# A two-layer transformer kernel on one core: the first stage's normalised tiles, latents' weights, weight splits and gate buffers are put in another order

## The reference, cut to what matters

```python
xn = _layernorm(x, axis=-1)                       # no weights
# attention latents (192 + 64 + rope columns), then a layernorm of each
q_latent = _layernorm(xn @ q_a_w.T, ...)
kv_mixed = xn @ kv_a_w.T
# feed-forward: rms norm of xn, router (32 experts, top 4), shared part
x2 = w_norm * (xn * rsqrt(mean(xn * xn) + eps))
logits = x2 @ w_router
sh = silu(x2 @ sw_gate) * (x2 @ sw_up) @ sw_down  # 704 hidden columns
```

## Time and profile before

| | |
|---|---|
| Time, median of 3 runs | 721.2 us (719.69 to 723.97) |
| The profiled execution | 723.6 us, its span 721.8 us |
| PE / PEld | 687.2 us (95%) / 583.5 us (81%) |
| DVE / ACT / POOL | 498.0 (69%) / 404.5 (56%) / 284.6 us (39%) |
| PE in 0 to 8.8 us and 8.8 to 11.5 us | 0.00 and 1.92 us busy |
| PE in 67 to 107 us | 39.84 us busy |

### The profile page before, as it was taken

One profiled execution on the slowest core, in us unless ns is written; L12 is line 12 of the kernel. 1 busy time (PEld: TensorE's weight loads), 2 busy tenths in 40 slices (PEclk: granted clock), 3 DMA queues, 4 the chain that ended last, 5 costly groups with the idle time before them and its releaser, 6 DMA issues.

```text
span 721.8 us, 13707 instructions
## 1 busy us (share of the span) xinstructions
PE 687.2 (95%) x4708; PEld 583.5 (81%) x4708; DVE 498.0 (69%) x1440; ACT 404.5 (56%) x1062; POOL 284.6 (39%) x289
## 2 busy tenths in 40 slices
PE   4999999999999999998999979999979999999997
PEld 2677888888888888887876655666779999999997
DVE  5798877877868778777884895777555454644544
ACT  2666158788788878788112565888753322222221
POOL 0473245556465454631004208998233230400000
PEclk9999999999999999999999986999999999999999
DMA  8902034453534444352800000200300000000000
GB/s 319 334 0 82 16 108 133 150 169 113 174 114 164 128 141 136 101 156 93 360 0 1 1 2 1 103 2 2 118 1 1 2 1 15 1 15 1 2 16 15
DMA packets 26724, 59.42 MB, mean 82 GB/s; under 512 B 3146, under 2 KB 12748, under 8 KB 26272
## 3 DMA queue, kind: packets, MB, share of 16 engines
q1 hardware_dynamic: 23584, 50.35, 20.7%
q0 software_dynamic: 3072, 8.20, 3.4%
HBM read 48.24 MB, written 10.49 MB: 81 GB/s over the span
## 4 chain that ended last, share of the span: by engine, by line
PE 75%; DVE 15%; ACT 5%; issue 3%; DMA 1%; POOL 1%; SPq 0%; DVEq 0%; ACTq 0%
PE bank L2155 10%; PE bank L1935 7%; PE bank L1869 6%; PE bank L1926 5%; PE bank L2204 5%; PE bank L2178 5%; PE bank L1955 3%; PE bank L1876 3%; PE bank L1946 3%; PE bank L2066 3%; PE bank L2124 3%; PE bank L2108 3%; PE bank L1997 3%; PE bank L2218 2%; PE bank L2090 2%
## 5 line engine op out<-in xcount | busy, mean ns | idle before, releaser
L1030 ACT ACTIVATE sb<-bank,sb 128x256 f32<-128x256 f32 x128 | 59.4, 470 | 40.5 <-DVE sb L1482 35.2
L1482 DVE TENSOR_REDUCE sb<-bank 128x2 f32<-128x512 f32 x64 | 43.7, 683 | 47.6 <-PE bank L1935 47.2
L1935 PE MATMUL bank<-sb 128*128 128x256 f32 x256 | 66.1, 381 | 0.0
L1713 DVE TENSOR_TENSOR sb<-sb,bank 128x256 f32<-128x256 f32 x56 | 23.5, 420 | 61.7 <-ACT sb L1153 61.7
L2155 PE MATMUL bank<-rounded,b_hi 128*128 128x256 f32 x224 | 63.5, 284 | 0.0
L2155 PE MATMUL bank<-am_lo,b_hi 128*128 128x256 f32 x224 | 63.4, 283 | 0.0
L2155 PE MATMUL bank<-rounded,b_lo 128*128 128x256 f32 x224 | 63.4, 283 | 0.0
L1187 ACT ACTIVATE h_parts<-sb 128x256 fp32r<-128x256 f32 x56 | 23.4, 418 | 70.8 <-DVE sb L1722 42.5
L1129 ACT ACTIVATE sb<-sb 128x128 f32<-128x128 f32 (+1 forms) x128 | 50.7, 445 | 18.1 <-DVE sb L1683 18.1
L1153 ACT ACTIVATE sb<-bank 128x256 f32<-128x256 f32 x56 | 21.4, 383 | 65.8 <-PE bank L2155 65.8
L1037 ACT ACTIVATE sb<-sb 128x256 f32<-128x256 f32 x128 | 57.7, 503 | 0.1
(11 more groups left out here) (301 smaller groups left out, 1946.3 us busy)
## 6 DMA issues: line engine op xcount, KB each, us to landing
sb<-in_w_gate_up SPq DMA_DIRECT2D x32, 368.0 KB
sb<-in_w_down SPq DMA_DIRECT2D x32, 256.0 KB
sb<-in_w_pair SPq DMA_DIRECT2D x8, 704.0 KB
expert_out<-sb SPq DMA_DIRECT2D x1, 4096.0 KB, 22.6
sb<-expert_out SPq DMA_DIRECT2D x8, 512.0 KB, 6.9
sb<-in_w SPq DMA_DIRECT2D x1, 1792.0 KB, 14.2
sb<-in_b SPq DMA_DIRECT2D x1, 1792.0 KB, 7.4
sb<-in_sw_up SPq DMA_DIRECT2D x1, 1536.0 KB, 9.4
```

Source lines behind the costliest of these rows:

```text
L1030: act.activation(probs[:, u % 4, q, :], bank[3 + u % 2][:, q * S:(q + 1) * S], ACT.Exp, scale=-1.0, bias=row_min[:, u % 4, q:q + 1], accum ...
L1482: dve.tensor_reduce(row_min[:, u % 4, :], bank[3 + u % 2][:, :].rearrange("p (q n) -> p q n", q=QT), AX.X, ALU.min).then_inc(at_min, 1)
L1935: mm = pe.matmul(bank[3 + u % 2][:, q * S:(q + 1) * S], qb[i][:, h, b * S + q * P:b * S + (q + 1) * P], keys[:, h, b * S:(b + 1) * S], sta ...
```

## The change

Four things are altered, and the third buffer brings one new wait.

1. On DVE, the first four tiles are normalised as soon as their own statistics are done; the statistics of the other four tiles come after them. On ACT the second root of the deviation moves behind the first two copies of turned tiles.
2. On SP, `w_lat` is issued before the third and fourth pair of x instead of after them.
3. On ACT, the three splits of `sw_up` are done at tiles 3, 4 and 5 instead of 3, 5 and 7.
4. `sgate` and `sup` have three buffers (`u % 3`), the third in region 4, in the place that the weights of the first attention pairs are loaded to later. So SP waits for all twelve products (`sh_h`, 12) before it loads those.

```diff
-        sgate, sup = r2.take(2, CH), r2.take(2, CH)
+        sgate, sup = ([part[:, i] for i in range(2)] for part in (r2.take(2, CH), r2.take(2, CH)))
...
+        sgate.append(r4.take(CH))
+        sup.append(r4.take(CH))
...
                 if i == 1:
                     sp.dma_start(cf[:, 0:CF_FIRST], t["consts"][:, 0:CF_FIRST]).then_inc(cf_in, 16)
-            sp.dma_start(w_lat, t["w_lat"]).then_inc(lat_in, 16)
+                    sp.dma_start(w_lat, t["w_lat"]).then_inc(lat_in, 16)
...
             sp.wait_ge(rt_dest, 1)
+            sp.wait_ge(sh_h, 2 * NF)
             for i in range(2):
                 pair_weights(i, i)
...
-                pool.tensor_tensor(hT[0:n, u // 2, (u % 2) * CH:(u % 2 + 1) * CH], sgate[0:n, u % 2, :], sup[0:n, u % 2, :],
+                pool.tensor_tensor(hT[0:n, u // 2, (u % 2) * CH:(u % 2 + 1) * CH], sgate[u % 3][0:n], sup[u % 3][0:n],
                                    ALU.mult).then_inc(sh_h, 1)
...
-            for h in range(2):
+            def deviation(h):
                 half = slice(h * HALF, (h + 1) * HALF)
                 act.wait_ge(ln_var, h + 1)
                 act.activation(sd[:, half], var[:, half], ACT.Sqrt).then_inc(ln_sd, 1)
+
+            deviation(0)
...
             for g in range(2):
                 turned_copy(g, xnT)
+            deviation(1)
...
-                if i % 2 and i > 1:
+                if 3 <= i < 3 + SU_STEPS:
 
                     act.wait_ge(shared_in, 48)
-                    act.activation(r(su_step(su_hi, i // 2 - 1)), su_step(sw_up, i // 2 - 1), ACT.Copy).then_inc(su_high, 1)
+                    act.activation(r(su_step(su_hi, i - 3)), su_step(sw_up, i - 3), ACT.Copy).then_inc(su_high, 1)
...
-                if u >= 2:
-                    act.wait_ge(sh_h, u - 1)
+                if u >= 3:
+                    act.wait_ge(sh_h, u - 2)
...
             statistics(range(HALF))
             variance(0)
-            statistics(range(HALF, HALF + 2))
             inverse(0)
-            normal(0)
-            normal(1)
-            statistics(range(HALF + 2, NT))
+            for i in range(HALF):
+                normal(i)
+            statistics(range(HALF, NT))
             variance(1)
-            normal(2)
             inverse(1)
-            normal(3)
```

More of the change, by code:

```diff
@@ L983, in shared_hidden @@
                     n, up = FH, bank[2 * (u % 2)][FH:2 * FH, :]
-                act.activation(sgate[0:n, u % 2, :], bank[2 * (u % 2)][0:n, :], ACT.Silu).then_inc(sh_act, 1)
-                act.activation(sup[0:n, u % 2, :], up, ACT.Copy).then_inc(sh_act, 1)
+                act.activation(sgate[u % 3][0:n], bank[2 * (u % 2)][0:n, :], ACT.Silu).then_inc(sh_act, 1)
+                act.activation(sup[u % 3][0:n], up, ACT.Copy).then_inc(sh_act, 1)
             for u in range(2):
```

## The result

The change makes the kernel 0.64% faster: 719.43 us against 721.34 (medians of 20 runs each), ratio of the runs 0.9936 with the interval 0.9911 to 0.9962, which is 4.6 us of 721, or 2.7 to 6.4. The two medians alone lie only 1.9 apart. The reason is in the runs themselves: seven of the twenty after the change took 712.4 to 713.9, two 716.3 and 717.8, and eleven 719.3 to 720.7, and their mean granted clock was 0.990 in the first group, 0.983 in the second, 0.981 in all but one of the third. The profiled execution is one of the third group, 720.73 with a span of 718.9, where before it was 723.60. So at the end 2.9 us are left in the pair of traces.

A forecast was written before the change was run, and what follows sets the result against it. PE, busy 687 of 722 us, bounds the kernel, so only starting its dense part sooner helps. 2.6 + 1.8 + 0.6 = 5.0 us off the median 721.2 gives 716.2 us, range 712.8 to 720.4.

The forecast's parts named there:

- the sum: First stage, end of DVE's row: early start 2.6, L1299 1.8 and product overlap 0.6 make 5.0 us.
- The chance of faster: Whole kernel: a time below 717.6, more than half a percent faster, given 0.61; within half a percent 0.32, slower 0.07.
- The early tiles, "2.6 us": Kernel start: earlier tiles and w_lat let PE's latents start at 8.95 instead of 11.57, 2.6 us sooner.
- the case of 9.04: Kernel start: if w_lat still landed at 9.04, latents start at 9.35 and 2.2 us are left.
- The clock at the start, ends 1.1 and 3.7: PE's first latents: clock rise moves with the work, keeping 2.6 us; 1.1 if it stays at 16, 3.7 if still sooner.
- The upper end: PE's first latents: clock rises still sooner, turns wait for DVE's 12.9, third tile starts at 13.7, 3.7 us sooner.
- L1299, "1.8 us": DVE's latents' variance: with sooner splits POOL's low parts end at 26.5, before L1299 at 27.3, gaining 1.8 us.
- The third buffer, "0.6 us": DVE's router comparison L1359: POOL's product of u = 7 starts sooner, so it waits 0.6 and not 1.2, gaining 0.6 us.
- The takeover: End of DVE's row, where PE starts the fifth turned tile of latents and turns dense: 62.2 instead of 67.16.
- it carries to the end: After the takeover: PE waits only for engines whose work moves with it, so the 5.0 us reach the end.
- the rivals: Clock rises no sooner, 718.0 (0.15); products meet DVE worse, 719.4 (0.13); little arrives, 720.3 (0.10); lower clock through latents, 724.4 worst (0.05).
- rivals that put a smaller gain down to the first stage: First stage: clock rises no sooner, gain 3.2 (0.15); products meet DVE worse, 1.8 (0.13); little arrives, 0.9 (0.10).

The follow-up runs named there:

- experiment 5: The changed kernel unaltered, run again on another chip; 719.37 us (12 runs), ratio 0.9953 to the kernel before.
- experiment 1: The kernel before with only DVE's and ACT's new order at the start, w_lat still behind all of x; 717.52 us in one execution, PE's takeover at 64.24.
- experiment 2: The kernel before with only w_lat's issue moved ahead of x's third pair; 721.06 us in one execution, PE's takeover at 67.75.
- experiment 4: The changed kernel with two gate buffers and without SP's wait for the twelve products; 714.72 us in one execution, PE's takeover at 62.64.
- experiment 3: The changed kernel with the sw_up splits back at tiles 3, 5 and 7; 718.91 us in one execution, PE's takeover at 62.54.
- experiment 7: The changed kernel with 13 unused matmuls in PE's pauses between 420 and 427 us; 711.04 us (6 runs), ratio 0.9858 to the kernel before.
- experiment 6: The changed kernel with 13 unused matmuls at PE's start, ahead of the first turn; 718.00 us (12 runs), ratio 0.9938 to the kernel before.
- experiment 9: The kernel before with unused matmuls at the start (17), at 331 to 340 and 420 to 427 us; 713.25 us, ratio 0.9870 to it without them.
- experiment 10: The changed kernel with unused matmuls at the start (13), at 331 to 340 and 420 to 427 us; 708.11 us, ratio 0.9799 to the kernel before.
- experiment 11: The kernel of experiment 10 with 17 wider bf16 matmuls in the pauses of 511 to 523 us; 707.55 us, ratio 0.9785 to the kernel before.

## Why the prediction was right, and where it was not

**The range and the sign held; the size was given by terms of which some were right for another reason.** The prediction said 716.2, within 712.8 to 720.4. The mean of the 20 runs is 717.2, their median 719.4. That the runs gave 4.6 where the sum said 5.0 is in part luck: the same two kernels gave 0.47% or 3.4 us in experiment 5, as each set of runs draws its low-clock stretches. (The chance of faster adds up to 0.62, 0.57 and a third of 0.15, and not to the 0.61 given; nothing hangs on it.)

*The early tiles, "2.6 us".* Right in size: the latents started 2.7 sooner (8.86), the third tile 2.62 sooner (14.77, predicted 14.8). Four tiles were done at 7.50, the turns ran 7.00 to 8.94 (6.8 to 8.95 predicted), the later tiles were done at 12.66 (12.9). But the step gave w_lat a part: "If w_lat still landed at 9.04 they would start at 9.35, and 2.2 be left." Experiment 1 shows that the order alone gives 2.6 at the latents' start and w_lat's move 0.1. There w_lat landed at 8.57 in its old place, and the turns end at 8.86 anyway; the case of 9.04 didn't occur with the new order. Alone the move costs 0.6 (experiment 2). This term belongs to DVE's order.

*The clock at the start, ends 1.1 and 3.7.* The forecast kept the rise moving with the work. The pair of traces shows this (5.20 against 5.10 for the eight records), but in part by luck: of traces with the same code up to there, three took 5.17 to 5.21 (the change, experiments 4 and 5), the others 4.25 (experiment 3) and 3.64 (experiment 7). The Trainium skill ("TensorE: Matmul & The Clock Gate", Part 1: The HAM clock gate), cited for the spread from run to run, is borne out by these rows. The upper end was real: the third tile starts 4.25 sooner than before in experiment 7, with no help, and 4.7 sooner in experiment 6's one trace.

*L1299, "1.8 us".* Right: 29.86 to 27.25 (27.3 predicted), and 0.18 instead of 1.94, so 1.76. POOL's low parts ended at 26.36 (26.5 predicted). Experiments 3 and 9 show the other side, 1.94 and 1.95 with the later splits. The splits fell where predicted (18.19 against 18.2) and cost PE nothing.

*The third buffer, "0.6 us".* Right place, mis-sized for the comparison: the product of u = 7 ended at 50.06, ahead of L1362 at 50.13, so that the whole overlap went (1.02, not 0.6). Of this 0.16 was paid elsewhere on DVE's row: 0.87 net by experiment 4. The predicted gaps of PE in the shared units are gone, and SP's first load of a pair was issued at 61.33; neither was on the path, as said.

*The takeover:* predicted 62.2, measured 61.88; 5.28 us instead of 5.0. DVE's row from L1302 to it is 34.6 long; the prediction said about 35.

*"Behind that PE waits only for engines whose work moves with it, so it carries to the end."* **This is the step that failed**, for the profiled execution and for the median. Experiments 9 and 10 show that the statement on the engines is true: with the clock nearly held, 5.1 come out in the time of the runs. What it left out is that PE's own speed isn't fixed. The first paragraph of the prediction called PE "at the full granted clock in nearly every slice"; but that row has an 8 and a 6 among its nines, and the stretches show some 24 us at half clock in three places (340.1 to 343.5, 428.9 to 445.9, 538.1 to 541.5), and every execution draws them anew. The profiled execution lost 2.4 to such a draw. None of the rivals named it; the margin "the median of three runs 4.3 apart is uncertain by a us or more" saw its trace and took it for noise. All of the rivals that put a smaller gain down to the first stage were wrong on the place: there the forecast was met.

What stays open: why the change draws the lowest group more often (18 of 32 against 10 of 34) isn't shown. Whether the fixed distance of its pauses to the start does it, or chance, these runs can't tell.

## What to carry to other kernels

Read the granted clock as a timeline and not as a mean: each slice under 9 has PE's pauses ahead of it, and some 60 short matmuls in those pauses, whose result nobody reads, were worth more here (11.9 us by the medians, 9.7 by the means, and runs within 0.6 of each other) than the change in question (5.1). When a change moves the work of a kernel with such pauses, follow its lead along the trace, from the place where it arises to the end, and compare runs at like mean clock, before saying that it was worth more or less than its sum. The instruction on few elements that took 2 us on DVE (L1299) stood behind one of POOL's: here it was POOL's work that had to be moved in front, not DVE's.

## What the runs showed that was not expected

- Pauses of PE between 0.5 and 2.2 us, several in a row, were followed by 3.4 us at a granted clock of 0.50 in some executions and by none in others of kernels with the same pauses (experiment 4 beside the change).
- In the long stretch from 426 us PE stayed at that level for 17.1 us though it was busy for 19.8 of 22 us; in experiment 4 for 10.2 us. With thirteen matmuls of 128 columns ahead of it it stayed at 1.00 in every execution that was traced (experiments 7 to 11).
- A run's time is set by these draws in groups: 712.7, 717.8 and 720.0, in both sets of runs of the change.
- w_lat's transfer of 418 KB took 4.9 us in the place ahead of the third pair, and landed at 7.15; behind that pair it landed at 9.04 before and at 8.57 in experiment 1, with the same bytes ahead of it.
- The Trainium skill ("SBUF — State Buffer", Who interferes with whom) has the second of the two fully blocked until the first finishes, where a VectorE instruction has two SBUF inputs and the GpSimd instruction reads SBUF. Experiment 4 agrees to 0.15 us: the product began 0.11 ahead and lasts 1.29, which would hold the comparison up for 1.18, and it took 1.03 longer.
